# Attention rows turned earlier and copied by VectorE, and an activation table loaded ahead of a copy, in a one-core transformer layer

## The reference

```
e     = emb[id];  h = e + 0.1 * mask * layernorm(gelu(cat(gelu(e Wi), gelu(geo[id] Wg), gelu(vis[id] Wv)) Wf))
x2    = layernorm(h)
h     = h + bf16(softmax(q k^T / 4) v) Wo + bo      (4 heads of 16, within a sequence, D = 64)
x3    = layernorm(h);  w = x3 . wr + br
y     = gelu_tanh(x3 W1 + b1) W2 + b2               (hidden 256)
out   = h + x3 + (w * y for the 511 tokens of highest w of each row, else nothing)
```

## Time and profile before

| | |
|---|---|
| time, median of 3 runs | 567.49 us (566.33 to 568.15) |
| the profiled execution, its own time | 562.24 us |
| its span, first to last instruction | 560.4 us |
| PE busy | 472.5 us (84%) |
| DVE busy | 447.6 us (80%) |
| ACT busy | 389.6 us (70%) |
| POOL busy | 339.3 us (61%) |
| mean granted clock of PE | 0.937 of full speed |

### The profile page before, as it was taken

One profiled execution on the slowest core, in us unless ns is written; L12 is line 12 of the kernel. 1 busy time (PEld: TensorE's weight loads), 2 busy tenths in 40 slices (PEclk: granted clock), 3 DMA queues, 4 the chain that ended last, 5 costly groups with the idle time before them and its releaser, 6 DMA issues.

```text
span 560.4 us, 16306 instructions
## 1 busy us (share of the span) xinstructions
PE 472.5 (84%) x5636; PEld 365.3 (65%) x5636; DVE 447.6 (80%) x1881; ACT 389.6 (70%) x662; POOL 339.3 (61%) x410
## 2 busy tenths in 40 slices
PE   0677687999999999999999999999999898977753
PEld 0345465777777777777777777777777676755643
DVE  1367657788888888888888888988888887887787
ACT  0425555888888888787788788887888786854740
POOL 5467345666666666666666676666666666321564
PEclk9989889999999999999999999999999998997555
DMA  3112011011111111111111111111111111000244
GB/s 102 22 24 35 14 23 24 11 20 21 23 23 23 23 23 23 23 23 23 23 23 22 19 19 20 18 20 19 23 23 23 23 23 23 1 2 3 77 112 112
DMA packets 23717, 15.81 MB, mean 28 GB/s; under 512 B 18832, under 2 KB 21520, under 8 KB 23568
## 3 DMA queue, kind: packets, MB, share of 16 engines
q0 software_dynamic: 6144, 9.97, 12.3%
q1 hardware_dynamic: 17552, 5.58, 3.7%
HBM read 11.08 MB, written 4.19 MB: 27 GB/s over the span
## 4 chain that ended last, share of the span: by engine, by line
PE 45%; ACT 23%; issue 15%; DVE 6%; POOL 5%; another core or an unknown queue 2%; DMA 2%; ACTq 1%; DVEq 0%; POOLq 0%; SPq 0%
ACT prob L469 7%; PE psum L856 6%; PE psum L864 6%; PE psum L800 5%; PE psum L885 4%; PE psum L943 4%; ACT hid L462 4%; PE psum L908 4%; PE psum L883 3%; ACT L469 3%; ACT o_t L409 3%; ACT L462 3%; PE psum L920 2%; PE psum L871 2%
## 5 line engine op out<-in xcount | busy, mean ns | idle before, releaser
L309 POOL TENSOR_TENSOR rs<-ve,minus_half 128x4 f32<-128x4 f32 x96 | 99.5, 1036 | 130.9 <-DVE ve L524 129.7
L301 POOL DMA_INDIRECT G<-table,idx x128 | 125.2, 978 | 39.9 <-issue 34.6
L613 DVE TENSOR_REDUCE neg_max<-psum 128x4 f32<-128x512 f32 x128 | 84.8, 685 | 7.4 <-PE psum L856 6.1
L469 ACT ACTIVATE prob<-psum 128x512 f32<-128x512 f32 x128 | 69.7, 613 | 2.6 <-PE psum L818 2.2
L776 PE MATMUL psum<-wt,hid 128*128 128x64 f32 x512 | 67.5, 289 | 1.1 <-ACT hid L462 1.1
L529 DVE TENSOR_SCALAR x<-R,mv,rs 128x64 f32 (+1 forms) x256 | 65.9, 323 | 1.5 <-POOL rs L309 1.5
L776 PEld LDWEIGHTS psum<-wt,hid 128*128 128x128 f32 x512 | 64.6, 205 | 1.5 <-ACT hid L462 1.4
L943 PE MATMUL psum<-x3t,wt 64*128 64x256 f32 x256 | 39.7, 432 | 16.8 <-issue 9.5
L462 ACT ACTIVATE hid<-psum,wt 128x512 f32<-128x512 f32 x64 | 40.5, 683 | 9.4 <-PE psum L943 9.1
L856 PE MATMUL psum<-k_s,q_s 32*128 32x128 f32 x1024 | 38.0, 285 | 10.6 <-ACT prob L469 9.8
L462 ACT ACT_TABLE_LOAD x31 | 39.8, 1283 | 8.5 <-PE psum L943 8.1
(11 more groups left out here) (109 smaller groups left out, 1044.2 us busy)
## 6 DMA issues: line engine op xcount, KB each, us to landing
out<-R SPq DMA_DIRECT2D x11, 256.0 KB, 2.7
G<-table,idx POOLq DMA_INDIRECT x128
wt<-packed SPq DMA_DIRECT2D x1, 1028.0 KB, 4.8
out<-R SPq DMA_DIRECT2D x2, 512.0 KB, 3.9
q_s<-max_t SPq DMA_DIRECT2D x32, 8.0 KB
out<-R SPq DMA_DIRECT2D x2, 128.0 KB, 2.6
ids_sb<-ids SPq DMA_DIRECT2D x1, 64.0 KB, 1.9
```

The source lines that it names most:

```text
L301: pool.indirect_dma_start(G[par][:, b, :], None, table, bass.IndirectOffsetOnAxis(ap=idx[par][:, b:b + 1], axis=0),).then_inc(gathered[par ...
L309: pool.tensor_tensor(rs[:, :], ve[:, :], minus_half[:, :], ALU.pow).then_inc(S[dst], 1)
L469: act.activation(prob[:, :, h, :], bank[h].rearrange("p (b q) -> p b q", b=GB), ACT.Exp, scale=SCALE).then_inc(S["prob_ready"], 1)
L613: dve.tensor_reduce(neg_max[:, GB * h:GB * h + GB], bank[h].rearrange("p (b k) -> p b k", b=GB), AX, ALU.max, negate=True).then_inc(S["max ...
```

## The change

Three things. ACT gets a one-element activation `loaded` with Gelu_apprx_tanh before it waits for `x3t_ready`, so that the table load of `hid` comes there, ahead of the copy `x3t`. The four turns of `attention_t` go from behind the scores (L818) to behind the turn of `x3` (L920) on PE, and write bank 0 in place of bank 5; they wait for `max_t`, which empties bank 0. The copy `o_t` goes from ACT (between the first and second `prob`) to DVE, behind the statistics that follow `fused`. The second scores wait for this copy, since they write bank 0; the turn of `gv` no longer waits for it.

```
-            def attention_out(e):
-                wait(act, "ot_ready", 1, e)
-                ends(act, "wo_ready", 1, e - 1)
-                act.activation(o_t[:, :], bank[5][:, 0:GT // 2].bitcast(BF16), ACT.Copy
-                               ).then_inc(S["o_t_ready"], 1)
...
                 if on(d):
+                    act.activation(loaded[:, :], w["b_q"][0:1, :], ACT.Gelu_apprx_tanh)
                     wait(act, "x3t_ready", 1, d)
                     act.activation(x3t[:, :], bank[ffn_bank(d) + 1][:, 0:2 * P], ACT.Copy
...
-                if on(e) and late(i):
-                    attention_out(e)
...
-                    if h == 0 and on(e) and not late(i):
-                        attention_out(e)
...
                     stats(lambda s: ft[:, s, :], st1, "st1_ready", a)
+                if on(e):
+                    wait(dve, "ot_ready", 1, e)
+                    dve.tensor_copy(o_t[:, :], bank[0][:, 0:2 * P].bitcast(BF16)
+                                    ).then_inc(S["o_t_ready"], 1)
...
             def attention_t(e):
-                ends(pe, "o_ready", 1, e)
-                wait(pe, "t1_ready", 1, e + 3)
+                wait(pe, "o_ready", 1, e)
+                wait(pe, "max_t_ready", 1, e + 1)
                 for s in range(GB):
-                    last = mm(bank[5][:, s * P // 2:(s + 1) * P // 2].bitcast(BF16),
+                    last = mm(bank[0][:, s * D:(s + 1) * D].bitcast(BF16),
...
-                    wait(pe, "o_t_ready", 1, a - 4)
                     mm(bank[5][0:GB * VD, 0:P], gv[:, :, :].rearrange("p b d -> p (b d)"), ident,
...
                     last.then_inc(S["x3t_ready"], 1)
+                if on(e):
+                    attention_t(e)
                 if on(e) and late(i):
-                    attention_t(e)
                     project(e)
...
                     wait(pe, "max_row_in", 16, c)
+                    wait(pe, "o_t_ready", 1, c - 1)
                     wait(pe, "qs_ready", 1, c + 1)
...
-                if on(e) and not late(i):
-                    attention_t(e)
```

More of the change, by code:

```diff
@@ L140, in build @@
         hid = sb("hid", [P, 2, GT])
+        loaded = sb("loaded", [1, 1])
         wt_rank = sb("wt_rank", [P, P])
```

## The result

| | before | after |
|---|---|---|
| median of the runs side by side | 567.82 us (566.33 to 569.12) | 585.17 us (579.28 to 596.86) |
| ratio | | 1.0229, 95% interval 1.0166 to 1.0293 |
| in a second set of runs (below) | 565.11 us | 580.07 us (575.39 to 582.13), ratio 1.0271 (1.0219 to 1.0323) |

The change makes the kernel slower by 2.3 to 2.7%, 13 to 15 us, where +21.3 was forecast; 585.17 lies in the range of 577 to 604. Among the profiled executions the spans are 560.4 us before, 586.2 after, and 577.9 in the second set. Two of the first four executions of after, 588.04 (the profiled one) and 596.86, were disturbed and slower than the others, so the ratio leaves them out, and for the whole span the second set's profile counts; within the loop both profiles have the same two kinds of step.

What follows compares the result with a forecast made beforehand. Bound: one ring through ACT and PE, 14.85 us a step. Terms +1.16 + 0.16 - 0.48 = +0.84, over 26 steps +21.8, with -0.5 at the edges +21.3: 588.8 us on the median, range 577 to 604.

Steps and rivals of the forecast that it cites:

- the ring of ACT and PE: Loop step's chain, ACT from x3t to last prob, PE from scores to q: 14.85 us, forecast to grow by 0.84.
- The load ahead of x3t: On ACT from q_s's end to x3t: load and one-element activation make 1.50, less 0.34 of wait, +1.16 a step.
- Behind x3t: On ACT from x3t's end to hid: 1.58 after the change, waiting for PE's product, so +0.16 a step.
- the second kind of step shows that time bare: Before's steps where hid waited 0.28 for PE behind its load; their 1.58 was taken as the wait for the product.
- The copy off ACT: Copy o_t leaves ACT's place between prob: last prob ends 0.48 sooner after hid; on DVE the copy takes 0.65.
- PE's side: Turns of o moved on PE: 0.24 to 0.40 less ahead of the scores, L933 0.40 later, their waits cost nothing.
- DVE does not decide: DVE's own ring with the copy and later L933 comes to 15.01 a step, below the 15.68 of ACT and PE.
- The edges: Steps outside the loop's rhythm: -1.3 in three written-out steps at the start, +0.8 at the end, together -0.5 us.
- The clock: Rival: PE's longer idle time ahead of L943 lowers its clock, 1.0 us more a step; 602 or 615; chance 0.14.
- DVE sets the step with the load hidden: Rival: x3 is turned late, ACT's wait hides the load, DVE's 15.01 sets the step; 571 us; chance 0.08.
- Faster: Rival: the wait between q_s and x3t hides the load and DVE its copy; 0.32 less a step, 558.7; chance 0.06.
- The load doubled: Rival: table lost between the one-element activation and hid, 1.3 more a step, 622 us; within the rest's 0.02 chance.

Runs made afterwards that it cites:

- second set of runs: The kernel after run once more with no edit: 580.07 us, ratio 1.0271 against before.
- the load alone: The kernel before plus only the one-element activation that puts the table load ahead of x3t; turns and copy o_t unmoved: 587.12 us, ratio 1.0386.
- the turns alone: The kernel after without the one-element activation, so both the turns and the copy o_t are moved: 596.47 us, ratio 1.055 against before.
- the copy alone: The kernel before with copy o_t moved to DVE, between rm1 and the update of R; turns in their old place, no load ahead: 554.71 us, ratio 0.9774.

## Why the prediction was right, and where it was not

The total and the side were right: a step of 15.69 was forecast, 15.62 and 15.79 were measured. But that the sum came so close is luck: the wait behind x3t was put 0.32 too high, late rises of 0.36 to 0.53 were left out, and the two errors cancel. Term by term, a loop step:

| term | forecast | measured |
|---|---|---|
| q_s's end to x3t | 1.50, so +1.16 | 1.41, so +1.07 |
| x3t's end to hid | 1.58, so +0.16 | 1.26, so -0.16 |
| o_t off ACT | -0.48 | prob 2.56 to 2.06, -0.50 |
| the ring of ACT and PE | +0.84 | +0.41 by these rows; +0.38 by steps (15.26 - 14.88) |
| rises that come late | nothing | +0.36 to +0.53 |

*The load ahead of x3t.* Right in place and mechanism. The one-element activation took 0.20 (estimate 0.16, bounds 0.06 to 0.27), but x3t overlaps it by 0.10 where I had added 0.04 of gaps. x3t has no idle time ahead of it in any of 20 steps of after, so PE's turn was never the later of the two.

*Behind x3t.* The step that failed in size: "the second kind of step shows that time bare". It doesn't. The product's last rise comes 1.18 behind its first instruction in 14 of the 21 loop steps of before, and in after and the load alone; in that second kind of before it comes at 1.48 to 1.58, once at 2.30. The one step of that kind with 1.18 is the one whose gathers came later (at 423.26 us). What I took for the bare time of the product held a late rise of 0.3. The bound of 1.32 was the better value, and even it held the load. With 1.26, the load alone is +1.07 - 0.16 = +0.91, and it measured +0.87.

*The copy off ACT.* The size was right on ACT, and on DVE it took 0.41 to my 0.65, near the lower bound of 0.42 that o gave, so in these rows the time went with the bytes read (0.42 for as many bytes of f32) and not with the number of elements (0.75 for k_s).

*PE's side, the step whose mechanism was missing.* "So these waits cost nothing", and "L933 comes 0.40 later": I priced the turns by what they occupy on PE. PE did lose nothing by them, its pause ahead of L938 being 1.34. What they cost is the announcement. With them between x3's turn and fused's, ft rises 0.84 or 2.12 behind its end, where it was 0.2 to 0.3. The chain from there, each link in the rows above: statistics and o_t 0.96 or 2.25 late; in the steps with 2.25 the scores wait 0.19 for o_t, and PE 0.78 for R; 0.97 together, the difference between 15.21 and 16.22. In the steps with 0.96 nothing comes of it. The forecast had named a sign of being wrong that fits here, that the last prob no longer frees the scores. In the steps of 16.22 it doesn't: the last prob ends at 312.29, PE is busy until 312.44 (L836), and L850 follows with no idle time. In the steps of 15.21 the prob still frees them, by 0.16, and not by the 0.3 to 0.5 of the forecast.

*"DVE does not decide"* was thus wrong in every second step. My sum of DVE's ring had 15.01 against 15.68, 0.67 to spare, and a release 2.25 late takes more than that. The place of the copy, behind the late wait, passed the lateness on to the scores; in the turns alone, where no load slows the ring, that was worse (18.8 us of waits ahead of L812).

*The edges.* Forecast 26 steps of +0.84 and -0.5 at the edges. On the spans, 577.9 - 560.4 = 17.5, of which the 23 distances of the loop hold 23 x 0.74 = 17.0. All the rest gave +0.5, where the forecast had 3 x 0.84 - 0.5 = +2.0 for it.

*The rivals.* The clock: false in after, where a pause of 1.34 in every step left the clock at 1.00 with the product at 1.13; true of the turns alone, where a pause of 1.61 stood ahead of the scores and the clock granted from 310 to 315 us was 0.56. *DVE sets the step with the load hidden*: false, the load was never hidden. *Faster*: false as put (and its 0.32 a step holds only for a load that is hidden whole; with the wait of 1.46 the condition beside it gives 0.28), but its argument, that ACT's copy is on the ring and DVE has room, is what the copy alone bore out; the load was the wrong companion for it. *The load doubled*: false, three loads a step as before. The Trainium skill's drain of about 1380 ns (page "ScalarE: Activation LUTs", section "What ACT_TABLE_LOAD costs") again does not show: 0.01 to 0.02 lies between the load of 1.28 and what follows it.

*Shown and not shown.* Shown: the load costs 0.87 a step by itself; with the moved turns PE's rises come later than before; it isn't PE's pause; they come on time with a quarter of the gathers, and in after itself in the step whose gathers are issued later; without SyncE's transfer the statistics wait less; the order of the turns decides who is late. Not shown: what part of the chip spaces the rises by 0.7 us, and whether the result itself is late or only its announcement, since the records of the instructions end on time and are modelled. The clock's fall in the turns alone stands behind the longer waits and was not separated from them. A version with the gathers issued later in every step was not tried; the one step that has it says that it is worth trying.

## What to carry to other kernels

A table load is free only beside work that it doesn't delay: ask what the engine releases next, not whether the engine waits somewhere. An instruction moved on a queue can cost more than its duration where its neighbours' releases come late; in the trace of before, compare the end of each neighbour's record with the start of what waits for it (x3t started 0.4 behind a finished turn), and put no further release in between. Where a change has several parts, time each: here one part, the copy moved to another engine, won 2.3% (with the turns in their old place), and the two beside it lost more than that. And before an experiment is built, look through the loop for a step that differs in just the suspected thing: here one step with late gathers already told the cause.

## What the runs showed of the hardware that was not expected

- While several gathers issued by GpSimd were in flight, semaphores of PE rose up to 2.3 us behind the end of the instruction that raises them, in order and about 0.7 us apart; with one gather in place of four, and in the step of after whose second gather was issued at 1.12, they rose 0.01 to 0.02 behind it. In the first step of after in the table, DVE's semaphore for k_s rose on time (1.72, its record ending at 1.70), and ACT's for x3t released PE within 0.05.
- With no other change, taking out one small transfer by SyncE (16 rows of 128) changed before by nothing (0.9999) and the turns alone from 1.055 to 0.987.
- An activation of one element took 0.20 us, and a copy of 128 x 512 bf16 out of PSUM took 0.41 on DVE against 0.59 on ACT.
- A pause of PE of 1.34 us in each step of 15.2 to 16.2 left the granted clock at 1.00; in the turns alone a pause of 1.61 ended at 309.17, and the clock granted from 310 to 315 us was 0.56.
